# Cross-attention with a routed FFN on one core: where the column sums of the second batch are made

## The reference

```
q1 = fake_quant(layernorm(x));  q2 = fake_quant(ctx)     # 8-bit grids, scale and zero point
x1 = x + q1 @ q2                                         # per batch, 512x1024 by 1024x1024
y  = layernorm(x1)
p  = softmax(y @ W_router.T); top 2 of 8 experts -> combine
out = x1 + y @ W_base.T + b + 2 * sum_e combine_e * (y @ A_e.T) @ B_e.T
```

## Time and profile before

| what | value |
|---|---|
| time, median of 3 runs | 168.48 us (168.28 to 168.65) |
| profiled execution: its own time | 168.88 us |
| profiled execution: its span | 167.1 us |
| TensorE matmuls busy | 155.1 us, 93% of the span |
| DVE busy | 127.4 us, 76% |
| ScalarE busy | 72.6 us, 43% |
| GpSimd busy | 37.9 us, 23% |
| chain that ended last, share of TensorE | 60% |

### The profile page before, as it was taken

One profiled execution on the slowest core, in us unless ns is written; L12 is line 12 of the kernel. 1 busy time (PEld: TensorE's weight loads), 2 busy tenths in 40 slices (PEclk: granted clock), 3 DMA queues, 4 the chain that ended last, 5 costly groups with the idle time before them and its releaser, 6 DMA issues.

```text
span 167.1 us, 2467 instructions
## 1 busy us (share of the span) xinstructions
PE 155.1 (93%) x875; PEld 80.5 (48%) x875; DVE 127.4 (76%) x283; ACT 72.6 (43%) x96; POOL 37.9 (23%) x113
## 2 busy tenths in 40 slices
PE   6858889879999999999999999999999999999990
PEld 3324335425446654644564456445644564555540
DVE  7988668999999989999889875988485828607702
ACT  3266699869999873225005300800080008003000
POOL 8204150343000433040614153125300040000000
PEclk9999999999999999999999999999999999999998
DMA  5999999991798523605430903291327002700311
GB/s 100 367 418 409 412 409 408 408 410 63 218 330 263 201 52 74 177 16 158 95 63 4 234 17 63 48 173 34 63 46 205 4 0 44 209 0 0 129 63 65
DMA packets 23677, 26.94 MB, mean 161 GB/s; under 512 B 17776, under 2 KB 18032, under 8 KB 23664
## 3 DMA queue, kind: packets, MB, share of 16 engines
q1 hardware_dynamic: 23520, 26.78, 50.8%
q10 hardware_dynamic: 144, 0.00, 0.0%
HBM read 18.38 MB, written 4.19 MB: 135 GB/s over the span
## 4 chain that ended last, share of the span: by engine, by line
PE 60%; DVE 12%; DMA 10%; ACT 9%; SPq 3%; issue 2%; POOL 2%; DVEq 0%; POOLq 0%
PE ps L889 37%; PE ps L840 10%; DMA xs<-in_x 7%; PE ps L877 6%; ACT w_hi L412 5%; DMA stage<-in_ctx_kv 3%; DVE w_lo L625 2%; SPq L208 2%; PE ps L868 2%; PE ps L870 2%; PE ps L869 2%; ACT a L366 1%; DVE a L556 1%; DVE ar_lo L619 1%; SPq L203 1%
## 5 line engine op out<-in xcount | busy, mean ns | idle before, releaser
L889 PE MATMUL ps<-w_hi,yt_hi 128*128 128x512 f16 x128 | 38.3, 380 | 0.9 <-ACT w_hi L412 0.9
L889 PE MATMUL ps<-w_hi,yt_lo 128*128 128x512 f16 x128 | 38.2, 379 | 0.0
L889 PE MATMUL ps<-w_lo,yt_hi 128*128 128x512 f16 x128 | 37.2, 379 | 0.0
L840 PE MATMUL ps<-a,a_t 128*128 128x512 f16 x128 | 30.1, 379 | 2.2 <-ACT a L366 0.9
L366 ACT ACTIVATE a<-stage,prm,inv_s 128x1024 uint8<-128x1024 f32 x16 | 19.5, 1241 | 9.5 <-DMA stage<-in_ctx_kv 9.2
L447 ACT ACTIVATE gate<-gate,ar_undo 128x1 f32<-128x1 f32 x8 | 2.4, 295 | 46.5 <-DVE gate L661 46.5
L840 PEld LDWEIGHTS ps<-a,a_t 128*128 128x128 f16 x128 | 12.2, 98 | 16.8 <-ACT a L366 1.4
L889 PEld LDWEIGHTS ps<-w_hi,yt_lo 128*128 128x128 f16 x128 | 12.5, 98 | 15.1 <-DVE yt_lo L638 0.2
L889 PEld LDWEIGHTS ps<-w_lo,yt_hi 128*128 128x128 f16 x128 | 12.5, 98 | 14.1
L889 PEld LDWEIGHTS ps<-w_hi,yt_hi 128*128 128x128 f16 x128 | 11.5, 98 | 15.0 <-issue 2.1
L293 POOL TENSOR_SCALAR root<-mvy 128x1 f32<-128x1 f32 x8 | 1.9, 234 | 57.7 <-DVE mvy L514 57.7
(11 more groups left out here) (138 smaller groups left out, 248.1 us busy)
## 6 DMA issues: line engine op xcount, KB each, us to landing
stage<-in_ctx_kv SPq DMA_DIRECT2D x16, 512.0 KB, 5.5
stage<-in_w_t SPq DMA_DIRECT2D x8, 512.0 KB, 13.0
xs<-in_x SPq DMA_DIRECT2D x7, 512.0 KB, 12.0
out_dram<-xs SPq DMA_DIRECT2D x7, 512.0 KB, 3.0
ar_raw<-in_ar_t SPq DMA_DIRECT2D x1, 544.0 KB, 13.7
xs<-in_x SPq DMA_DIRECT2D x2, 256.0 KB, 3.8
b_raw<-in_b_t SPq DMA_DIRECT2D x1, 512.0 KB, 12.5
bias_sb<-in_bias SPq DMA_DIRECT2D x1, 512.0 KB, 13.3
```

What stands on the lines that cost most here:

```text
L840: last = nc.tensor.matmul(ps[:, s1_bank(t) + h, :], a1_t[:, t % 4, k, :], a2[:, k, h * H:(h + 1) * H], start=k == 0, stop=k == K - 1)
L889: ins = nc.tensor.matmul(ps[:, OUT_BANK[p] + h, :], part, rhs[:, k, h * H:(h + 1) * H], start=k == 0 and i == 0, stop=stop and i == 2)
```

## The change

1. The 16 matmuls of `column_sums` for batch 1 go. Instead SP issues a DMA transpose (`turn_ctx`) of each of the eight quantised context tiles into the slot of `stage` that its floats have left. Four of them stand right after the last context load, one between the transposes of `y_hi(2)` and `y_lo(2)`, three between `y_lo(2)` and `a1(4)`.
2. ScalarE sums the turned tiles along their free dimension (`sum_columns`, eight activations of 1024 elements with an accumulator). The first of them waits for all eight turned tiles. TensorE spreads the sums over the partitions (`spread_columns`: four f32 matmuls of 128 columns each with a broadcast column, twice), inside `wide(2)` after steps 1 and 4; ScalarE makes `corr` of batch 1 in two halves from that.
3. ScalarE's order: `y_hi(2)` before the last context tile, `gate_weight(1)` before `hct(0)`, the last context tile after `y(2)`.
4. DVE's order: `gate_tile(1)` before `split_hct(0)`, and the statistics and the quantisation of x tile 4 later. `add_corr` of tiles 1, 2 and 3 leaves DVE: GpSimd adds `corr` to `xs` (`correct_x`) after the tile's quantisation and ahead of its product, two of them in front of `scale_y(0)`, the third behind it. `sum_x1` waits for that. `add_corr(0)` and those of tiles 4 to 7 stay on DVE.

The diff, without its declarations of semaphores and tiles:

```diff
+        def turned_ctx(k):
+            return stage[:, k, 0:H].bitcast(F16).rearrange("p (j r) -> p j r", j=K)
...
+            def turn_ctx(n):
+                sp.wait_ge(ctx_ready, n + 1)
+                sp.dma_start_transpose(turned_ctx(n - K), a2[:, n - K, :]).then_inc(ctx_turned, 16)
+
             for n in range(K, N):
                 load_ctx(n)
+            for n in range(K, K + 4):
+                turn_ctx(n)
             transpose_y_hi(2)
+            turn_ctx(K + 4)
             transpose_y_lo(2)
+            for n in range(K + 5, N):
+                turn_ctx(n)
             transpose_a1(4)
...
+            def correct_x(t):
+                pool.wait_ge(corr_ready, 1)
+                pool.wait_ge(x_quantised, t + 1)
+                nc.gpsimd.tensor_tensor(xs[:, t, :], xs[:, t, :], corr[:, 0, :], ALU.add).then_inc(x_corrected, 1)
...
             scale_x(2, 4)
+            correct_x(1)
+            correct_x(2)
             scale_y(0)
+            correct_x(3)
             scale_y(1)
...
+            def make_later_corr(h):
+                act.wait_ge(columns_spread, h + 1)
+                nc.scalar.activation(corr[:, 1, h * H:(h + 1) * H], ps[:, SPREAD_BANK, :], ACT.Identity,
+                                     bias=col_bias, scale=col_scale).then_inc(corr_ready, 1)
...
+            def sum_columns(j):
+                act.wait_ge(ctx_turned, 16 * K)
+                act.wait_ge(rows_summed, 2)
+                if j > 1:
+                    act.wait_ge(columns_summed, j - 1)
+                turned = stage[:, :, 0:H].bitcast(F16).rearrange("p k (j r) -> p k j r", j=K)
+                nc.scalar.activation(junk[:, j % 2, :].rearrange("p (k r) -> p k r", k=K), turned[:, :, j, :],
+                                     ACT.Copy, accum_out=col_sum[:, j:j + 1]).then_inc(columns_summed, 1)
...
-            for n in range(K + 6, N):
-                quantise_ctx(n)
+            quantise_ctx(K + 6)
             make_y_hi(2)
+            gate_weight(1)
             split_hct(0)
             make_y(2)
-            gate_weight(1)
+            quantise_ctx(K + 7)
+            split_hct(1)
             sum_row(1)
-            split_hct(1)
-            make_corr(1)
-            for t in range(2, T):
+            for j in range(5):
+                sum_columns(j)
+            gate_weight(2)
+            sum_columns(5)
+            make_y_hi(3)
+            make_y(3)
+            make_later_corr(0)
+            sum_columns(6)
+            sum_columns(7)
+            split_hct(2)
+            make_later_corr(1)
+            sum_row(2)
+            for t in range(3, T):
                 gate_weight(t)
...
             def first_half_y(t):
+                if 0 < t < TB:
+                    dve.wait_ge(x1_summed, t + 1)
...
                 dve.wait_ge(x_quantised, t + 1)
+                if 0 < t < TB:
+                    dve.wait_ge(x_corrected, t)
...
             make_first_y()
-            add_corr(1)
             first_half_y(1)
...
-            add_corr(2)
             statistics_y(2)
             gate_tile(0)
             split_b()
-            statistics_x(4)
+            gate_tile(1)
             split_hct(0)
             make_y_lo(2)
-            gate_tile(1)
+            split_hct(1)
+            statistics_x(4)
+            add_bias(0)
+            sum_out(0)
             quantise_x(4)
-            add_bias(0)
-            split_hct(1)
-            sum_out(0)
-            add_corr(3)
             statistics_y(3)
             centre_a1t(4)
...
+            def spread_columns(h):
+                pe.wait_ge(columns_summed, 4 * h + 4)
+                if h == 1:
+                    pe.wait_ge(corr_ready, 2)
+                for i in range(4):
+                    j = 4 * h + i
+                    last = nc.tensor.matmul(ps[:, SPREAD_BANK, i * P:(i + 1) * P],
+                                            col_sum[:, j:j + 1].to_broadcast([P, P]), ident[:, :],
+                                            start=True, stop=True)
+                last.then_inc(columns_spread, 1)
...
             def late_product(t):
                 pe.wait_ge(a1t_ready, t + 1)
-                pe.wait_ge(corr_ready, 2)
...
             lora(0, stop=True)
-            for k in range(K):
-                column_sums(1, k)
-                if k == 3:
-                    transpose_hc(1)
+            transpose_hc(1)
             lora(1, stop=True)
...
                     wide(t, k, k == K - 1)
+                    if t == 2 and k == 1:
+                        spread_columns(0)
+                    if t == 2 and k == 4:
+                        spread_columns(1)
```

More of the change, by code:

```diff
@@ L76, in xattn_ffn @@
         y_hi = sb("y_hi", [P, D], F16)
+        col_sum = sb("col_sum", [P, K], F32)
         y_lo = sb("y_lo", [P, D], F16)
@@ L140, in xattn_ffn @@
         COLSUM_BANK = 6
+        SPREAD_BANK = 3
         WARM_BANK = 5
@@ L163, in xattn_ffn @@
         colsum_done, corr_ready = sem("colsum_done"), sem("corr_ready")
-        x1_ready = sem("x1_ready")
+        x1_ready, x_corrected = sem("x1_ready"), sem("x_corrected")
         rows_summed = sem("rows_summed")
@@ L179, in xattn_ffn @@
         yt_hi_in, yt_lo_in = [sem(f"yt_hi_in{i}") for i in range(2)], [sem(f"yt_lo_in{i}") for i in range(2)]
-        a1t_in = sem("a1t_in")
+        a1t_in, ctx_turned = sem("a1t_in"), sem("ctx_turned")
+        columns_summed, columns_spread = sem("columns_summed"), sem("columns_spread")
         ar_done = sem("ar_done")
@@ L367, in quantise_ctx, with make_first_corr @@
                                      bias=prm[:, 3:4], scale=inv_s[:, 2:3]).then_inc(ctx_ready, 1)
-            def make_corr(b):
-                act.wait_ge(colsum_done, b + 1)
-                nc.scalar.activation(corr[:, b, :].rearrange("p (h n) -> p h n", h=NH),
+            def make_later_corr(h):
+                act.wait_ge(columns_spread, h + 1)
+                nc.scalar.activation(corr[:, 1, h * H:(h + 1) * H], ps[:, SPREAD_BANK, :], ACT.Identity,
+                                     bias=col_bias, scale=col_scale).then_inc(corr_ready, 1)
+            def make_first_corr():
+                act.wait_ge(colsum_done, 1)
+                nc.scalar.activation(corr[:, 0, :].rearrange("p (h n) -> p h n", h=NH),
                                      ps[:, COLSUM_BANK:COLSUM_BANK + NH, :], ACT.Identity,
                                      bias=col_bias, scale=col_scale).then_inc(corr_ready, 1)
+            def sum_columns(j):
[6 more added lines that the diff above has]
+                                     ACT.Copy, accum_out=col_sum[:, j:j + 1]).then_inc(columns_summed, 1)
             def sum_row(t):
@@ L380, in sum_row @@
                     act.wait_ge(rows_summed, t - 1)
+                    act.wait_ge(columns_summed, K)
                 nc.scalar.activation(junk[:, t % 2, :], a1[:, t, :], ACT.Copy, bias=-OFFSET - MIDDLE,
@@ L461, in _ @@
             act.wait_ge(consts_ready, 2)
-            make_corr(0)
+            make_first_corr()
             peak_of_first_w()
@@ L504, in add_corr @@
                 dve.wait_ge(x1_summed, t + 1)
-                dve.wait_ge(corr_ready, t // TB + 1)
+                dve.wait_ge(corr_ready, 1 if t < TB else 3)
                 nc.vector.tensor_tensor(xs[:, t, :], xs[:, t, :], corr[:, t // TB, :], ALU.add).then_inc(x1_ready, 1)
-                dve.wait_ge(x1_ready, t + 1)
+                dve.wait_ge(x1_ready, 1 if t == 0 else t - 2)
             def first_half_y(t):
+                if 0 < t < TB:
+                    dve.wait_ge(x1_summed, t + 1)
                 nc.vector.bn_stats(bny[:, t, 0, :], xs[:, t, 0:H])
```

## The result

| | before | after |
|---|---|---|
| time, median (runs) | 168.56 us (4) | 182.29 us (4: 180.69 to 182.94) |
| profiled execution / its span | 168.88 / 167.1 us | 180.69 / 178.9 us |
| mean granted TensorE clock, profiled execution | 0.997 | 0.968 |

The ratio is 1.080, with a 95% interval of 1.072 to 1.088: 13.7 us slower, where 4.8 were forecast. The profiled execution of after is the fastest of its four; the pair of traces has 11.8 us to explain, and what makes the other three 1.2 to 2.3 longer no trace shows. Two positions divide the 11.8. The first `w_hi`, on ScalarE, starts 6.48 us later (42.37 for the 35.89 of the earlier trace rows), and `narrow(3)` 12.45 later (98.58 for the 86.13 of the earlier trace rows). So 6.5 us arise ahead of `w_hi`, 6.0 between there and tile 3, and behind it 0.6 comes back.

What follows compares the result with a forecast made beforehand. It took the kernel as bound by a chain through VectorE and ScalarE's w_hi up to 45 us, and by TensorE from the first wide steps. 168.48 + 3.2 (turned sums) + 1.6 (adds) gave 173.3 us, range 170.0 to 177.5.

Steps and rivals of the forecast that it cites:

- Adds: Ahead of the first w_hi: GpSimd's adds and VectorE's passes shut each other out, so w_hi starts 1.6 us later.
- the first GpSimd add runs 25.4 to 27.6: Stage 1: the first add starts once VectorE's quantisations of tiles 2 and 3 end at 25.39.
- A later bullet of the prediction's list: Stage 1: scale_y(0) stands behind the second GpSimd add and starts at 31.0 instead of 28.92.
- some 1.6 more: Stage 1: extra cost on top of either end if the first add slips between the two quantisations.
- the third add in front of `make_first_y`: Stage 1: the third GpSimd add also goes ahead of make_first_y, another 2.2 us, making the adds' upper end +3.8.
- the clock (2.2): In wide(2): TensorE's clock falls while it idles; a start at the 1.2 GHz level had cost 2.2 us in warm-up.
- rival 2: Costs come harder: third GpSimd add first or clock fall in wide(2); either 175.5 us, both 177.7; chance 0.18.
- Turned sums: In wide(2): the first spread waits for sums of late-landing turns and two spreads are added; tile 2 ends 3.2 us later.
- The gap may be too short: In wide(2): the argument against a clock fall while TensorE idles some 4.4 us.
- the row that the prediction names: TensorE's row with eight matmuls of 512 columns in 1.90 us, from which a wide step of six was put at 1.3.
- the adds run free: GpSimd's adds run beside VectorE unhindered, so only the turned sums cost: 171.4 us; chance 0.22.
- the sums are in time: In wide(2): all turns land by 66.2, tile 2 ends 1.2 us earlier, 167.0 us in all; chance 0.07.

Runs made afterwards that it cites:

- e1: The kernel before with one half of the change, GpSimd's three adds in place of VectorE's; 175.63 us, ratio 1.043.
- e2: The changed kernel with the three adds back on VectorE, so the turned sums and new order alone; 174.28 us, ratio 1.036.
- e3: The changed kernel with idle matmuls put into three of TensorE's long gaps; 178.66 us, ratio 1.061.
- e5: The changed kernel without its last three turns, the sums waiting for five turned tiles; 177.06 us, ratio 1.050.
- e6: The kernel before with six extra GpSimd instructions (adds and memsets) beside VectorE's w_lo passes; 172.12 us in one run.
- e12: e11 with the centring of tile 5 back behind gate 3 on VectorE; 169.84 us, ratio 1.007.
- e4: e2 with the two spreads moved later, behind steps 4 and 7 of wide(2); 180.95 us, ratio 1.070.
- e11: e8 reordered further, then tile 4's products one wide step later, split_hct(2) earlier, the second spread behind the last wide step; 173.59 us, ratio 1.026.
- e8: e4 with ScalarE's order in tile 2 mended, then tile 4's statistics and the quantisations earlier on VectorE; 172.68 us, ratio 1.024.

## Why the prediction was wrong

The direction was right and so were the places; both terms were too small, and the time is 5 us above the range.

- **Adds, 1.6 forecast, 6.5 measured** (7.2 as a median, e1). The step that failed is "the first GpSimd add runs 25.4 to 27.6", that is, behind both quantisations. The add was ready at 23.50, inside the first one, and took its turn before the second. A later bullet of the prediction's list held the wrong path too: `scale_y(0)` did not start late because it stands behind the second add (that ended at 29.06) but because it waited 2.74 for VectorE's statistics, which the first two collisions had made late. The text knew of it ("some 1.6 more"), of the third add in front of `make_first_y` (2.2) and of the clock (2.2), and took none of them: each stood as an end of the range or a rival of its own. They share a cause, though: of two that shut each other out, the one that is ready first goes first. All three races went GpSimd's way, two of them because VectorE's pass ahead was still running, the third by 0.07 us. The clock fell behind the wait that the first two made. 2.8 us at `make_first_y`'s start, 2.0 in it and 1.9 for the clock, less 0.2 on the way, make the 6.5. The range ended at 177.5, short of even "both" in rival 2 (177.7).
- **Turned sums, 3.2 forecast, 6.0 measured** (5.8 as a median, e2). With 6.48 taken off, the last turn landed at 71.7, not 70.6 (upper end 71.4): `y_lo(2)` left SP 0.5 later, 0.4 of it because the new order puts `gate_tile(1)` ahead of it on VectorE (the prediction looked at ScalarE's order alone), the turns behind it took 1.40 of the queue each instead of 1.23, and the last needed 4.13 to land, not 3.0. The first spread so came at 76.0 for 75.0, +1.0. The spread and the step behind it at the low clock, which this term held at nothing, added 1.5, the spreads' length (0.89 for 0.8 each) 0.2; the sum is 5.9.
- **The clock** was put into a rival at 2.2 for one place, `wide(2)`. It fell there and in stage 1, at 1.5 and 1.9 by the two stretches, 3.6 by e3's median. "The gap may be too short" was wrong. The 2.2 was worked out from the pace of the warm-up matmuls; the profile's granted clock reads 1.00 over them, so no granted clock bears the 2.2 out. The Trainium skill's page "TensorE: Matmul & The Clock Gate", Part 1, has the low clock as what TensorE falls back to when idle. Both falls agree: one came behind an idle stretch of 1.97, the other in one of 4.24.
- **What held:** `narrow(2)` 2.5 ahead for 2.8; a wait of 4.24 for 4.4 ahead of the first spread, though that is luck in part, since TensorE came to it 1.2 later than forecast and the sums were done 1.0 later; the second spread without a wait; sums at 1.04 for 1.1; the spread held by a ScalarE sum, and that by the last turns (e5). A `wide` step does take 1.3, but this does not follow from the row that the prediction names: six eighths of 1.90 are 1.4.
- **The rivals:** that the adds run free falls with e1 and e6; that the sums are in time was reached only by moving spreads and orders (e12), and still was not faster.

## What to carry to other kernels

Price work that is moved to GpSimd with every VectorE pass that it can meet (here those with two SBUF inputs and the fast ones), and give the race to whichever is ready first: outcomes that hang on one rule are summed, not spread over rivals. A queue with one late item sets when a whole set is complete, so place the last transfer of a set, not the first. To the price of a wait of several us that a change adds on TensorE, add the half-rate steps behind it.

## What was not expected of the hardware

- Within a run the clock fell to the low level in or behind each of TensorE's longest waits in tiles 2 and 3: 4.2 us (after, first spread), 4.7 (e2), 2.9 and 4.5 (e4) and 3.6 (e11, `lora(3)`, where it was at 0.50 from 101 to 107). Matmuls behind them ran at it; in e11 pairs of 512 columns took 1.22 and 1.05 for the usual 0.73 and 0.63. Behind e8's wait of 2.0 it stayed at 1.00, though in after it fell behind one of 1.97 in stage 1.
- A DMA transpose from SBUF to SBUF took more of the issuing queue with other DMAs under way: 1.23 alone, 1.40 as the last three of after, 1.89 (7.57 for four) as its first, while the context's last tiles were still being loaded. Whether the other transposes or the loads make the difference was not tried.
